# The first half of the ffn's r projection moves across a turn's end, with one VectorE mix and one GpSimd product, in two recurrent layers

## The reference

```python
xa = _ln(x, ln1_w, ln1_b)
sx = shifted(xa) - xa
xxx = einsum(tanh((xa + sx * maa_x) @ maa_w1), maa_w2)      # five mixes
xk, xw, xv, xr, xg = xa + sx * (maa_stack + xxx)
w = exp(-exp(time_decay + tanh(xw @ td_w1) @ td_w2))
r, k, v, g = xr @ Wr.T, xk @ Wk.T, xv @ Wv.T, silu(xg @ Wg.T)
# over the tokens, per head:  out = r (u k v + s);  s = k v + w s
x1 = x + groupnorm(out) * g @ Wo.T
xc = _ln(x1, ln2_w, ln2_b)
sx2 = shifted(xc) - xc
xk2 = xc + sx2 * ffn_maa_k
xr2 = xc + sx2 * ffn_maa_r
rr = sigmoid(xr2 @ Wfr.T)                                   # the projection that moves
kk = square(relu(xk2 @ Wfk.T))
return x1 + rr * (kk @ Wfv.T)
```

## Time and profile before

| | |
|---|---|
| median of 3 runs | 3314.48 us (3312.49 to 3315.53) |
| the profiled execution's own time | 3309.64 us |
| its span, first to last instruction | 3307.8 us |
| mean granted TensorE clock | 0.956 |
| layer L1 in the span | about 690 to 1420 us |
| layer L3 in the span | about 2570 to the end |
| TensorE busy | 2962.5 us |
| VectorE busy | 1982.4 us |

### The profile page before, as it was taken

The page is one execution under the profiler, slowest core; times in us unless marked ns, Lnnn a source line. Parts: engine busy times, 40 slices in busy tenths (PEclk is TensorE's granted clock), DMA queues, the critical chain, the costliest instruction groups (busy, mean ns, idle before and its releaser), DMA issues.

```text
span 3307.8 us, 54593 instructions
## 1 busy us (share of the span) xinstructions
PE 2962.5 (90%) x18304; PEld 2313.1 (70%) x18304; DVE 1982.4 (60%) x4864; ACT 1394.6 (42%) x3713; POOL 705.3 (21%) x484
## 2 busy tenths in 40 slices
PE   6888888868999999689999999999989789999986
PEld 6555555756888888586555555699989668888866
DVE  2777777338899999523454455500100588999993
ACT  0777777543343333253444444513221223333332
POOL 0010110014444444201000010000000244444440
PEclk9999999978999999799999999999999789999998
DMA  2100000213322223200000000300000333322230
GB/s 99 34 22 32 21 32 12 121 35 93 86 86 88 85 86 100 77 25 18 19 18 18 18 26 10 124 18 0 0 0 22 125 92 86 90 86 85 85 110 26
DMA packets 96306, 182.78 MB, mean 55 GB/s; under 512 B 10138, under 2 KB 87514, under 8 KB 92862
## 3 DMA queue, kind: packets, MB, share of 16 engines
q1 hardware_dynamic: 96190, 181.28, 17.6%
HBM read 171.34 MB, written 9.90 MB: 55 GB/s over the span
## 4 chain that ended last, share of the span: by engine, by line
PE 67%; issue 13%; DVE 13%; ACT 4%; POOL 1%; DMA 1%; DVEq 0%; SPq 0%; ACTq 0%; POOLq 0%
PE psum L467 17%; PE psum L272 11%; PE psum L1882 5%; PE psum L1765 5%; PE psum L1820 4%; PE psum L1783 4%; PE psum L1260 3%; DVE psum L666 3%; PE psum L458 2%; PE psum L474 2%; PE psum L1828 2%; DVE arena L689 2%; PE psum L248 2%; DVE arena L681 2%; PE psum L1272 2%
## 5 line engine op out<-in xcount | busy, mean ns | idle before, releaser
L467 PE MATMUL psum<-arena 128*128 128x200 f32 x4096 | 785.6, 351 | 84.9 <-DVE arena L845 33.3
L467 PEld LDWEIGHTS psum<-arena 128*128 128x128 f32 x4096 | 732.8, 200 | 173.3 <-issue 109.0
L1064 POOL TENSOR_TENSOR arena<-arena 128x800 f32<-128x800 f32 x256 | 455.6, 1780 | 512.3 <-DVE psum L666 512.2
L681 DVE TENSOR_TENSOR_SCAN arena<-arena,psum 128x808 f32<-128x808 f32 x256 | 470.1, 1836 | 59.6 <-PE psum L458 46.8
L272 PE MATMUL psum<-arena 128*128 128x200 f32 (+1 forms) x2048 | 351.6, 334 | 22.1 <-DMA arena<-L_w 20.3
L272 PEld LDWEIGHTS psum<-arena 128*128 128x128 f32 x2048 | 348.8, 191 | 23.1 <-DMA arena<-L_w 20.3
L1461 ACT ACTIVATE arena<-arena 100x361 f32<-100x361 f32 x512 | 299.9, 588 | 118.5 <-DVE arena L1372 113.2
L1046 POOL TENSOR_TENSOR arena<-arena 128x800 f32<-128x800 f32 x80 | 139.7, 1746 | 829.3 <-DVE arena L689 670.5
L2117 ACT ACTIVATE arena<-arena 100x361 f32<-100x361 f32 x256 | 153.1, 598 | 334.3 <-DVE arena L1978 332.3
L1372 DVE CUSTOM_DVE_ANT_0 arena<-psum,arena 100x361 f32<-100x361 f32 x512 | 254.2, 530 | 39.0 <-issue 34.6
L1978 DVE CUSTOM_DVE_ANT_0 arena<-psum,arena 100x361 f32<-100x361 f32 x256 | 135.6, 530 | 231.3 <-issue 231.2
(11 more groups left out here) (128 smaller groups left out, 4241.5 us busy)
## 6 DMA issues: line engine op xcount, KB each, us to landing
arena<-v_rows SPq DMA_DIRECT2D x512, 202.0 KB, 3.2
arena<-ctxT SPq DMA_DIRECT2D x32, 722.0 KB, 4.3
arena<-L_w SPq DMA_DIRECT2D x8, 1152.0 KB, 16.0
arena<-L_w SPq DMA_DIRECT2D x8, 1024.0 KB, 9.8
v_rows<-arena SPq DMA_DIRECT2D x32, 202.0 KB, 2.1
arena<-L_fc SPq DMA_DIRECT2D x4, 1024.0 KB, 7.9
arena<-L_pj SPq DMA_DIRECT2D x4, 1024.0 KB, 15.8
arena<-xT SPq DMA_DIRECT2D x4, 800.0 KB, 9.9
```

The lines of the kernel that those rows point to most:

```text
L467: mm = pe.matmul(chunk(bank, j), m.W[n][:, k, c * P:(c + 1) * P], src[:, k, :], start=k == 0, stop=k == C - 1)
L681: dve.tensor_tensor_scan(m.ring[n % 4].rearrange("p j e -> p (j e)"), m.we[:, cc].rearrange("p j e -> p (j e)"), m.kv, 0.0, ALU.mult, ALU. ...
L1064: pool.tensor_tensor(sv, sv, rb, ALU.mult).then_inc(sem("r_states"), 1)
```

## The change

In TensorE's program the first half of the r projection no longer closes a turn: it stands in the next turn, behind the mean of norm 1 and ahead of `reduce(6)`. The second half stays where it was, behind `reduce(6)`. In VectorE's program the mix xr2 stands right behind the fifth mix, ahead of step 14. In ScalarE's program both tanh stand together near the start of the next turn. GpSimd's product 13 waits for VectorE's product 15 (it waited for product 14).

```diff
--- before.py
+++ after.py
@@ -486,6 +486,13 @@
                 if tail:
                     pe.wait_ge(m.n2.lnv.sem, m.n2.lnv.at(t, 1))
                 m.n1.pe_mean(pe, lambda c: X[:, c, ds(g + 1, N)], f)
+            if tail:
+                wait(pe, "ffn_mix", t, 8)
+                if rec:
+                    wait(pe, "mix_term", i, 20)
+                elif back:
+                    wait(pe, "bonus", b, 1)
+                project_half("fr", m.xr2, 0, 4, "ffn_r_sum")
             if back:
                 reduce(6, b)
             if tail:
@@ -630,13 +637,6 @@
                 if front:
                     wait(pe, "r", f, 1)
                 project_half("fk", m.xk2, 1, 3, "ffn_k_sum")
-
-                wait(pe, "ffn_mix", b, 8)
-                if front:
-                    wait(pe, "mix_term", f, 20)
-                elif rec:
-                    wait(pe, "bonus", i, 1)
-                project_half("fr", m.xr2, 0, 4, "ffn_r_sum")
 
         turns(pe, body)
 
@@ -838,12 +838,12 @@
                 if rec:
                     wait(dve, "gate_sum", i, 2)
                 mix_term(4)
-
-            step(14)
             if back:
                 for c in range(C):
                     dve.scalar_tensor_tensor(seq(m.xr2)[:, c], seq(m.sx2)[:, c], vec("ffn_maa_r", c),
                                              m.xs2[:, c, :, 1:E], ALU.mult, ALU.add).then_inc(sem("ffn_mix"), 1)
+
+            step(14)
 
             step(15)
 
@@ -890,8 +890,10 @@
                 wait(act, "decay_rate", i, 4)
                 decay(i, 1)
             if tail:
-                wait(act, "ffn_r_sum", t, 2)
-                act.activation(half(m.thr, 1), full(5), ACT.Tanh, scale=0.5).then_inc(sem("ffn_tanh"), 1)
+                wait(act, "group_done", t)
+                for h in range(2):
+                    wait(act, "ffn_r_sum", t, h + 1)
+                    act.activation(half(m.thr, h), full(4 + h), ACT.Tanh, scale=0.5).then_inc(sem("ffn_tanh"), 1)
 
             start(3)
             if front:
@@ -1030,9 +1032,6 @@
                     act.activation(half(m.ff, h), full(2 + h), ACT.Relu).then_inc(sem("ffn_relu"), 1)
                     wait(act, "ffn_relu", b, h + 1)
                     act.activation(half(m.kk, h), half(m.ff, h), ACT.Square).then_inc(sem("ffn_squared"), 1)
-                wait(act, "ffn_r_sum", b, 1)
-                wait(act, "group_done", b)
-                act.activation(half(m.thr, 0), full(4), ACT.Tanh, scale=0.5).then_inc(sem("ffn_tanh"), 1)
 
         turns(act, body)
 
@@ -1061,6 +1060,8 @@
                 if front and n == 13:
                     add_token(4)
                 if rec:
+                    if n == 13:
+                        wait(pool, "kv", i, 16)
                     pool.tensor_tensor(sv, sv, rb, ALU.mult).then_inc(sem("r_states"), 1)
 
         turns(pool, body)
```

## The result

The change is faster: 3268.31 us median of 4 runs (3262.71 to 3274.95) against 3315.01 median (3312.49 to 3321.47) of the kernel before on the same chip, ratio 0.9857 [0.9833, 0.9881]. In a later comparison it had 3268.32 against 3309.93, ratio 0.9872 [0.9849, 0.9894]. The profiled execution took 3269.77 us (span 3268.0, granted clock 0.960), 39.9 less than that of before.

A forecast was written before the change was run, and what follows sets the result against it. TensorE, busy in 90% of the span, was taken to lose 33.3 us waiting for xr2; 50 us gained in two layers less 10 for slow groups gave 40, so 3274 us (3264 to 3281; wider range 3262 to 3292).

The forecast's parts named there:

- The wait for xr2: TensorE ahead of the first r half, 33.3 us in all: goes, as xr2 is done 2.9 us before it is wanted.
- From the k projection to the variance: Start of the k projection to norm 1's variance matmuls: 16.4 us, before 22.07, 18.08 and 20.69 in turns 1, 2, 3.
- Product 0: VectorE's first product of the next turn: meets GpSimd's product 14 and takes 2.45 us in place of 1.00.
- The edits that I took at nothing: Turns -1, 0 and 7 to 9: no gain or loss; in turn 0 product 15 loses its block, product 0 gains one.
- The two tanh: ScalarE, before the square for norm 1: both lie in 1.8 us of cover and cost nothing.
- Turn 6: Its end, with no norm 1 behind it: from the k projection 21.5 us in place of 24.67, gain 3.2.
- The clock: Slow groups behind the remaining 1.14 us wait, turns 2 to 6: three of five, 5.0 us per layer, 10 in all.
- The sum: Turns 1 to 6 of a recurrent layer: gain 25.0 us without slow groups, 50 in two layers, 40 after the clock.
- VectorE as the bound: Rival, recurrent turns: VectorE can only be busy for 93%, a turn is 80.2 us, time 3296; chance 0.10.
- GpSimd in the way: Rival: one more GpSimd block of 1.73 us ahead of scan 0, variance at 18.1, time 3291; chance 0.11.
- the wait that comes back at the variance: Rival "nothing moves": scan 0 stays, the wait returns whole at the variance, only the clock gains, 3311 us; chance 0.05.
- Slower by the clock: Rival: the lower clock follows both remaining waits of a turn, 2.6 us each, 63 against 50, 3327 us; chance 0.05.

The follow-up runs named there:

- filled version: The changed kernel with the decay's first projection done twice, just ahead of the 1.14 us wait: 3259.18 us; rerun 3255.78 beside the changed kernel's 3268.32.

## Why the prediction was right, point by point

The time and the mechanism came out as forecast: 39.9 us between the profiled executions, 40 forecast. By the medians it is 3268.3 against 3274: the forecast put the kernel 4.84 us above its profiled execution, as the kernel before had been, and it came out 1.5 below it. That the 40 was met to 0.1 us is luck: the two layers gained 2.9 us more than the whole did, and code that isn't touched took that much back in this execution.

*The wait for xr2.* Gone, and with it its slow group. The version with xr2's move alone has no such wait and the whole gain, so this is the cause. It need not go whole: with GpSimd's wait alone half of it stays, and the slow group goes all the same.

*From the k projection to the variance.* Forecast 16.4. Turn 1 had 890.91 - 874.47 = 16.44, turn 2 16.53, and TensorE waited for GpSimd at `reduce(6)` for 0.21 us in turn 1 and 0.29 in turn 2, 0.1 to 0.2 forecast. The turns 3 to 5 had 16.00 and no such wait, since VectorE and GpSimd gain on TensorE while that runs at the lower clock.

*Product 0.* 2.49 us beside GpSimd's product 14, 2.45 forecast from the earlier trace rows. I called this the price of the edit on GpSimd. It is a price that every version looked at pays somewhere: with only xr2 moved, product 15 takes 2.40 us; with product 14 held back, the copy takes 1.56. All of them have the same time, so here it costs nothing that the runs can tell.

*The edits that I took at nothing.* The turns -1 and 0 of L1 lasted 118.1 us together, 117.9 before, and the stretch from the row to the 16 matmuls of line 233 that follow the layer took 119.7 us, 119.9 before. The two tanh cost nothing either: the second ended at 1044.95, and the square for norm 1 waited until 1045.38 for the centring.

*Turn 6.* From the k projection to the row it was 1286.40 - 1266.17 = 20.23 us, 21.5 forecast: a gain of 4.4, not 3.2. Here the turn had a slow group ahead of it, and VectorE had caught up. In the filled version, without one, it is 1277.34 - 1255.92 = 21.42, the forecast.

*The clock, the term that was mis-sized.* I put three slow groups in five turns at 1.68 each, 5.0 us per layer. There are four, behind the same 1.14 us wait, at 1018.76 (above) and once in each turn that follows. But one costs less than its group. Such a turn is 62.41 us from variance to k projection and 16.00 from there on, a turn without it 60.98 and 16.53, a difference of 0.9; in turn 6, where a late scan 0 is caught up, it is only 0.2. The filled version gives the sum: from the k projection of turn 1 to the row it takes 1277.34 - 868.41 = 408.93 us with no slow group, the changed kernel 411.93. That is 3.0 us per layer for four slow groups.

*The sum.* From the k projection of turn 1 to the end of turn 6, L1 took 1303.69 - 870.40 = 433.29 us before and 1286.40 - 874.47 = 411.93 after. This is 21.4 per layer (L3 has 21.4 as well), 20 forecast. Without the slow groups, as in the filled version, it is 24.4, 25.0 forecast. So the turns were forecast 0.6 us too good and the clock 2.0 too dear. The two layers together exceed the 39.9 by 2.9 us: in this execution the attention layers before L1, which aren't touched, ended 3.8 us later, and the other stretches gave the rest back.

Of the rivals, VectorE as the bound (a turn of 80.2), GpSimd in the way (18.1 to the variance), and the wait that comes back at the variance are refuted by these lines: a turn of 78.4, 16.0 to 16.5 to the variance, and no wait of more than 0.3 us there. "Slower by the clock" had a true core: the 1.14 us wait is followed by a slow group in four of six turns now, where it was in one of six before.

What stays open is why the kernel with GpSimd's wait alone keeps the upper clock behind two waits of 1.14 and 1.47 us, while the changed one loses it behind a single one of 1.14, and why the changed one itself keeps it in turn 2 (941.23 us, 2.97 behind the same 1.14).

## What to carry to other kernels

Read why an operation that others wait for is late: here half of the wait was the block by GpSimd and half the place in the queue, and either cure alone brought the whole gain. The move of the r half, which names the change, brought just over half by itself and nothing on top of xr2's move. What a wait costs under a clock that changes is to be read from the length of whole turns, not from the slow group behind it, since the engines beside it catch up meanwhile. And where a short wait stays just ahead of slow matmuls, moving real work of TensorE into it is worth a try; here even useless work gained 12.5 us, while moving the small copy out of VectorE's way to the same wait gained nothing.

## What the runs showed of the hardware

- A TensorE wait of 1.14 us was followed by the lower clock for a good part of the next group (4.65 us for 16 matmuls in place of 2.97, granted clock 0.63) in four turns of a layer; one of 0.46 us at the same place in none; and filling it with 1.35 us of useless matmuls made such a turn 0.9 us shorter.
- The same 1.14 us wait was followed by the upper clock in turn 2 of the changed kernel, and in three turns of the version with GpSimd's wait alone, where 1.47 us of further waiting stood 18 us later. A wait alone does not decide.
- VectorE instructions with two SBUF inputs are drawn out beside GpSimd's: a product from 1.00 to 2.49 us, four mixes from 1.41 to 2.96, the scaling of the norm from 0.97 to 2.34. A copy of 128x8 within SBUF is too, from 0.15 to 1.56. Scans, with an operand in PSUM, kept 1.84 (1037.96, beside GpSimd's product of 1038.01).
- Who is drawn out turns on a few tenths of a microsecond: line 262 started 0.06 us ahead of GpSimd's product and took 0.97, with GpSimd's at 2.52; 0.26 us behind it, it took 2.34.
